# A fused attention and feed-forward layer: four engines' order inside one iteration laid out anew

## What is computed

```python
def layer(x):                      # heads: 16 of 32
    a = layernorm(x)
    Q, K, V = heads(a @ Wq.T + bq), heads(a @ Wk.T + bk), heads(a @ Wv.T + bv)
    scores = Q K^T / sqrt(32) - (i - j)      for j <= i, else -inf
    attn = softmax(scores) V @ Wo.T + bo
    x = x + layernorm(attn)
    xh = layernorm(x) @ hadamard(512)
    scale = clip(max|xh|, 1e-5) / 7          # per token
    xq = clip(round(xh / scale), -8, 7) * scale
    wq = ternary(weight) * mean|weight|      # per row
    return x + layernorm(xq @ wq.T)
```

## Time and profile before

| | |
|---|---|
| median of 3 runs | 1217.08 us (1214.96 to 1219.63) |
| profiled execution | 1213.31 us |
| its span | 1211.4 us |
| TensorE busy | 1100.2 us, 91% |
| VectorE busy | 1009.3 us, 83% |
| ScalarE busy | 702.7 us, 58% |
| GpSimd busy | 599.1 us, 49% |

### The profile page before, as it was taken

The page is one execution under the profiler, slowest core; times in us unless marked ns, Lnnn a source line. Parts: engine busy times, 40 slices in busy tenths (PEclk is TensorE's granted clock), DMA queues, the critical chain, the costliest instruction groups (busy, mean ns, idle before and its releaser), DMA issues.

```text
span 1211.4 us, 44874 instructions
## 1 busy us (share of the span) xinstructions
PE 1100.2 (91%) x18625; PEld 726.4 (60%) x18656; DVE 1009.3 (83%) x2558; ACT 702.7 (58%) x1494; POOL 599.1 (49%) x719
## 2 busy tenths in 40 slices
PE   5899999999999999999999999999999999999641
PEld 3566556666666666666566666666666666666320
DVE  5749998888988888899888888988888899887772
ACT  5454566666566566655666665566566655665431
POOL 2333545555454556555545555454556555445422
PEclk9999999999999999999999999999999999999875
DMA  9746665666666576566675656656575566654230
GB/s 271 165 110 138 124 130 136 159 138 136 134 125 137 142 146 153 125 136 138 122 145 137 159 134 137 136 125 132 142 149 145 131 137 138 124 129 102 72 70 36
DMA packets 204687, 161.81 MB, mean 134 GB/s; under 512 B 150432, under 2 KB 150688, under 8 KB 204384
## 3 DMA queue, kind: packets, MB, share of 16 engines
q1 hardware_dynamic: 199600, 141.34, 55.2%
q0 software_dynamic: 4880, 17.57, 4.1%
HBM read 40.87 MB, written 16.78 MB: 48 GB/s over the span
## 4 chain that ended last, share of the span: by engine, by line
PE 56%; DVE 32%; issue 7%; ACT 2%; SPq 1%; DMA 1%; POOL 1%; POOLq 0%; DVEq 0%; ACTq 0%
PE f_job L1281 42%; DVE f_bst L980 6%; PE f_st L1382 3%; DVE f_z L1058 3%; PE f_o L1399 2%; PE f_o L1404 2%; DVE f_o L970 2%; DVE f_inverse L972 2%; PE f_job L1426 2%; DVE f_rmax L948 2%; DVE f_x L1004 2%; DVE f_folded_x L1021 2%; DVE f_y L1012 2%; DVE f_y L1011 2%; DVE f_small L1006 1%
## 5 line engine op out<-in xcount | busy, mean ns | idle before, releaser
L469 POOL TENSOR_SCALAR_AFFINE_SELECT f_PT<-f_PT 64x512 f32<-64x512 f32 (+1 forms) x256 | 202.0, 810 | 68.6 <-ACT f_PT L635 42.8
L484 POOL TENSOR_TENSOR f_square<-f_stage 128x512 bf16<-128x512 f16 x128 | 130.8, 1044 | 130.7 <-ACT f_stage L613 117.5
L1281 PE MATMUL f_job<-f_xTh,f_wqh 128*128 128x256 f16 x512 | 140.8, 275 | 15.6 <-DVE f_wkl L809 14.4
L613 ACT ACTIVATE f_stage<-f_job,f_bias 128x256 f16<-128x256 f32 x256 | 106.0, 465 | 83.7 <-PE f_job L1281 76.9
L475 POOL TENSOR_TENSOR f_OTl<-f_o,f_OTh 128x256 f16<-128x256 f32 x128 | 86.3, 674 | 114.4 <-ACT f_OTh L653 113.6
L1281 PE MATMUL f_job<-f_xTl,f_wqh 128*128 128x256 f16 x512 | 140.2, 274 | 0.0
L1281 PE MATMUL f_job<-f_xTh,f_wql 128*128 128x256 f16 x512 | 140.2, 274 | 0.0
L1281 PE MATMUL f_job<-f_xTh,f_wkh 128*128 128x256 f16 x512 | 139.9, 273 | 0.0
L1281 PE MATMUL f_job<-f_xTh,f_wkl 128*128 128x256 f16 x512 | 139.8, 273 | 0.0
L1281 PE MATMUL f_job<-f_xTl,f_wkh 128*128 128x256 f16 x512 | 139.7, 273 | 0.0
L934 DVE SCALAR_TENSOR_TENSOR f_stage<-f_job,f_bias,f_stage 128x256 f16<-128x256 f32 x256 | 110.7, 474 | 29.5 <-ACT f_stage L613 27.5
(11 more groups left out here) (181 smaller groups left out, 3026.5 us busy)
## 6 DMA issues: line engine op xcount, KB each, us to landing
f_stacks<-f_stage SPq DMA_DIRECT2D x380, 128.0 KB
f_xin<-x SPq DMA_DIRECT2D x32, 512.0 KB, 4.6
f_x<-x SPq DMA_DIRECT2D x32, 512.0 KB, 4.0
out<-f_z POOLq DMA_DIRECT2D x32, 512.0 KB, 3.3
f_Vmix<-f_V SPq DMA_DIRECT2D x32, 256.0 KB, 3.2
f_Vmix<-f_V SPq DMA_DIRECT2D x64, 128.0 KB, 3.4
f_stacks<-rows_const SPq DMA_DIRECT2D x3, 512.0 KB, 7.8
f_stacks<-wqT SPq DMA_DIRECT2D x2, 512.0 KB, 6.0
```

Of the source, the lines that this page charges most:

```text
L469: nc.gpsimd.affine_select(out=d, in_=d, compare_op=ALU.is_ge, fill=0.0, base=odd * SUB, pattern=[[0, 4], [0, TP], [1, SUB]], channel_multi ...
L484: nc.gpsimd.tensor_tensor(square[:, 2 * m + pair, :], h, h, ALU.mult).then_inc(squared, 1)
L613: nc.scalar.activation(stage[:, 2 * m, g, :], bank("qk", g)[:, m * W2:(m + 1) * W2], ACT.Identity, bias=bias[:, m, g:g + 1]).then_inc(qk_h ...
L1281: mm = pe.matmul(dst, lhs[a](c), rhs[b](c), start=(n == 0), stop=(n == 3 * KC - 1))
```

## The change

It writes the loop bodies of SyncE, GpSimd, ScalarE and VectorE in another order. TensorE's list and all helpers stay as they are, so that every wait is the same and only its place in its engine's queue differs.

```diff
--- before.py
+++ after.py
@@ -411,23 +411,25 @@
             for s in range(STEPS - 1):
                 n, m, k = s + 1, s + 2, s - 1
                 max_rows(s)
+                if s < 2:
+                    load_rows(n)
                 if has(k):
                     load_res(k)
                 if has(m + 1):
                     load_front(m + 1)
-                if s < 2:
-                    load_rows(n)
+                if s:
+                    mix_values(s)
                 restack(n, 0)
                 restack(n, 1)
                 restack(n, 2)
                 if has(m):
                     turn_x(m)
-                mix_values(n)
                 if has(k):
                     turn_x2(k, 0)
                     turn_x2(k, 1)
 
             last = STEPS - 1
+            mix_values(last)
             max_rows(last)
             load_res(last - 1)
             turn_x2(last - 1, 0)
@@ -502,6 +504,8 @@
             for s in range(STEPS - 1):
                 n, m, k = s + 1, s + 2, s - 1
                 square_of(n, 0)
+                if s and has(k):
+                    heads_low(k, 2)
                 if has(k):
                     heads_low(k, 3)
                 if has(m):
@@ -518,15 +522,14 @@
                 if has(k - 1):
                     z_root(k - 1)
                 if has(s):
+                    heads_low(s, 0)
                     clear_future(s, 3)
-                    heads_low(s, 0)
                     heads_low(s, 1)
                 if has(k - 1):
                     finish_out(k - 1)
-                if has(s):
-                    heads_low(s, 2)
 
             last = STEPS - 1
+            heads_low(last - 1, 2)
             heads_low(last - 1, 3)
             clear_future(last, 0)
             clear_future(last, 1)
@@ -702,57 +705,60 @@
             keep_v(0, 1)
             for s in range(STEPS - 1):
                 n, m, k = s + 1, s + 2, s - 1
-                qk_high_part(n, 0)
                 if has(k):
                     invert(k, 3)
+                qk_high_part(n, 0)
+                if s:
+                    heads_high(k, 2)
                 qk_high_part(n, 1)
                 keep_max(s)
+                qk_high_part(n, 2)
                 if has(k):
                     heads_high(k, 3)
-                qk_high_part(n, 2)
+                if has(k - 1):
+                    round_levels(k - 1, 0)
+                qk_high_part(n, 3)
+                exps(s, 0, 0)
+                if has(k - 1):
+                    level(k - 1, 0)
+                exps(s, 0, 1)
                 if has(m):
                     front_norm(m, 0)
-                if has(k - 1):
-                    round_levels(k - 1, 0)
-                if has(m):
                     front_norm(m, 1)
-                qk_high_part(n, 3)
-                if has(k - 1):
-                    level(k - 1, 0)
-                exps(s, 0, 0)
-                exps(s, 0, 1)
+                    front_high(m)
                 if s == 0:
                     keep_ffscale()
-                    keep_tern()
-                if has(m):
-                    front_high(m)
                 exps(s, 1, 0)
                 exps(s, 1, 1)
                 if has(k - 1):
                     round_levels(k - 1, 1)
+                    keep_q(k - 1, 0)
+                if s == 0:
+                    keep_tern()
+                if has(k - 1):
                     level(k - 1, 1)
-                    keep_q(k - 1, 0)
                 invert(s, 0)
-                exps(s, 2, 0)
-                invert(s, 1)
                 if has(k - 1):
                     keep_q(k - 1, 1)
+                invert(s, 1)
+                exps(s, 2, 0)
+                heads_high(s, 0)
                 exps(s, 2, 1)
                 keep_v(n, 0)
-                if has(k):
-                    x2_high(k, 0)
-                    x2_high(k, 1)
-                heads_high(s, 0)
                 exps(s, 3, 0)
                 exps(s, 3, 1)
                 keep_v(n, 1)
+                if has(k):
+                    x2_high(k, 0)
+                invert(s, 2)
+                if has(k):
+                    x2_high(k, 1)
                 if has(k - 1):
                     norm_z(k - 1)
-                invert(s, 2)
                 heads_high(s, 1)
-                heads_high(s, 2)
 
             last = STEPS - 1
+            heads_high(last - 1, 2)
             keep_max(last)
             invert(last - 1, 3)
             heads_high(last - 1, 3)
@@ -1111,18 +1117,18 @@
                     front_stats(m)
                 if has(k - 1):
                     find_scale(k - 1, 0)
+                if s == 0:
+                    fold_bias()
+                qk_low_part(n, 2)
                 if has(m):
                     front_offset(m)
-                qk_low_part(n, 2)
+                if s < 4:
+                    weight_guard(s)
+                qk_low_part(n, 3)
                 if has(k - 1):
                     find_scale(k - 1, 1)
-                qk_low_part(n, 3)
-                if s == 0:
-                    fold_bias()
                 if has(k):
                     y_out(k, 0)
-                if s < 4:
-                    weight_guard(s)
                 if has(m):
                     front_low(m)
                 if has(k):
@@ -1131,32 +1137,31 @@
                 normalise(s, 0)
                 if has(k):
                     residual(k)
+                    fold(k, 0)
+                    fold(k, 1)
+                    fold_again(k, 0)
                 if has(k - 1):
                     scale_out(k - 1, 0)
-                if has(k):
-                    fold(k, 0)
-                    fold_again(k, 0)
-                    fold(k, 1)
-                    fold_again(k, 1)
-                if has(k - 1):
                     scale_out(k - 1, 1)
                     z_stats(k - 1)
                 if has(k):
+                    fold_again(k, 1)
+                maxima(n, 0)
+                keep_norms(n)
+                maxima(n, 1)
+                normalise(s, 1)
+                if has(k):
                     x2_low(k, 0)
-                normalise(s, 1)
-                maxima(n, 0)
-                maxima(n, 1)
-                keep_norms(n)
+                maxima(n, 2)
                 if has(k - 1):
                     z_columns(k - 1)
+                maxima(n, 3)
                 if has(k):
                     x2_low(k, 1)
-                maxima(n, 2)
-                maxima(n, 3)
                 split_max(n)
-                normalise(s, 2)
                 if has(k):
                     x_stats(k)
+                normalise(s, 2)
 
             last = STEPS - 1
             normalise(last - 1, 3)
```

## The result

| | before | after |
|---|---|---|
| median of the runs | 1216.7 us (4 runs beside the changed kernel) | 1178.1 us (1176.6 to 1181.4) |
| ratio, 95% interval | | 0.968 (0.965 to 0.971) |
| span of the profiled execution | 1211.4 us | 1177.6 us (its time 1179.3) |
| TensorE busy | | 1095.7 us, 93% |
| VectorE, ScalarE, GpSimd busy | | 84%, 60%, 50% |

What follows compares the result with a forecast made beforehand. TensorE was taken to wait for VectorE's unbroken queue, 1.74 us a step. Gains of 22.4 us (20 regular steps at 1.12), 4.4 (s = 2, 3) and 2.8 (boundary) make 29.6, from 1217.1 to 1187 us; range 1171 to 1208.

Steps and rivals of the forecast that it cites:

- The sign and the place: Faster, chance 0.80, by removing TensorE's wait at `values(n, 1)` for `scale_out` to empty its bank, 21.6 us in 29 waits.
- The folds and the start of the maxima: On VectorE, three folds take 2.04 us, the first `scale_out` starts at t0 + 7.58, `maxima(n, 0)` at t0 + 11.39.
- The present 0.46 stays in the sum: L1006 on VectorE still lasts 0.46 us over its best 0.148 us, as in its meeting with GpSimd's `clear_future(s, 2)`.
- the 0.23: Added to a regular step for GpSimd's clearings now falling on VectorE's folds: half of one clearing's 0.46 us.
- VectorE decides, by 0.13: At `out_product(k, 0)` VectorE is ready at 27.17 us, TensorE at 27.04, so VectorE sets the step at 33.48 us.
- rival A: TensorE alone decides the step, VectorE's queue is a little shorter and no meeting costs: 43.2 us gained, 1174 us, chance 0.12.
- The boundary steps: The 7 steps with softmax in more pieces gain 0.18 and 0.22 us each, 2.8 us together.
- s = 2 and s = 3: Two early steps also lose a longer wait for `scale_out`, since `weight_guard` moves: 2.15 + 2.2 = 4.4 us.
- Start and tail are unchanged: The first and last stretches of the kernel neither gain nor lose time.
- at nothing: SyncE's move of `mix_values` ahead of the next step's `restack` costs nothing, its reader coming only after t0.
- ScalarE, GpSimd: nothing: Moving the third head's parts, `x2_high` and `x2_low` later costs nothing, as long as ScalarE keeps its slack.
- Rivals B and C: VectorE pays for GpSimd meetings: B, two clearings, half given back, 1203 us, chance 0.20; C, four, slower, 1226 us, 0.11.

Runs made afterwards that it cites:

- run 3: The changed kernel with only both `scale_out` back at their old places among the folds: 1212.0 us, ratio 0.995.
- run 10: The changed kernel with both `scale_out` at their old places and GpSimd's clears of the third head cut from 64 to 4 columns of each block: 1188.9 us.
- run 4: The changed kernel with `normalise(s, 1)` ahead of both maxima again and `keep_norms` behind both: 1188.1 us, ratio 0.976.
- run 5: The changed kernel with SyncE's order of the kernel before, the rest as changed: 1173.4 us, ratio 0.965.
- run 6: The changed kernel with the last iteration's row of maxima issued ahead of the last `mix_values`, nothing else: 1175.0 us, ratio 0.966.
- run 8: The changed kernel with GpSimd's order of the kernel before, the rest as changed: 1179.4 us, ratio 0.970.
- run 1: The kernel before with the new order on VectorE alone: 1261.0 us, ratio 1.036.
- run 9: The kernel before with VectorE's new order and two of ScalarE's moves (both `front_norm`, both `x2_high`): 1214.5 us, ratio 0.997.
- run 2: The changed kernel with VectorE's order of before, the other three engines as changed: 1356.3 us, ratio 1.112.
- run 11: The changed kernel with one more `bn_stats` on VectorE in each iteration, ahead of the front's statistics: 1181.5 us, ratio 0.971.
- run 7: The changed kernel with the order of before in the first iterations alone, on VectorE, ScalarE and SyncE: 1181.6 us, ratio 0.970.

## Why the prediction was right, and where it was wrong

*The sign and the place*: right. The bank of `values(n, 1)` was the wait that fell, and runs 3 and 10 show that bringing the second `scale_out` forward is worth 0.5 us a step by its place alone, the maxima's order 0.47 (run 4).

*The folds and the start of the maxima*: the working of the three folds held (2.02 us against 2.04), and so did the distance from the first `scale_out` to `maxima(n, 0)`: 409.54 - 405.73 = 3.81 against 3.81.

*"The present 0.46 stays in the sum"* and the 0.23 added to it: this is the term that failed. `exps(s, 2, 1)` comes later, so the clearing no longer meets L1012 (0.15 instead of 0.61), and it starts behind a fold, so GpSimd pays. The prediction wrote that by the rule alone every clearing would stop a fold, and took half of one. But the rule of the Trainium skill that it names there (SBUF — State Buffer, section "SBUF: two separate sides") gives the ports to whichever starts first. Here the first fold was ahead by 0.54 us. The meeting that did become longer is another one, at the front's statistics: 0.82 where it was 0.51 before and the least of that line is 0.17. VectorE's way from one t0 (365.54) to the end of `qk_low_part(n, 2)` (392.27) is 26.73 us against a forecast of 27.12: 0.5 shorter up to the first maximum, 0.3 longer at the statistics; the other 0.2 I have not assigned.

*"VectorE decides, by 0.13"*: wrong, TensorE decides, though by no margin. Both arrive at `out_product(k, 0)` together, 26.79 us behind t0 (392.33 - 365.54), 0.06 us apart, and in all regular steps from s = 5 on but one (0.33) TensorE's idle time there is at most 0.14; forecast were 27.17 and 27.04. TensorE is 0.25 us earlier, mainly because the waits of 0.14 and 0.12 at `scores(n, 1)` and `scores(n, 3)` did not come. Where VectorE is 0.67 us earlier still, the step stays at 33.1 (run 5). The period forecast for a regular step was 33.48 before the 0.23; rival A said 33.09, and 33.02 to 33.11 came. Its sum of 43.2 us for the steady part stands against the measured 44.05. A margin of 0.13 us was smaller than what one meeting with GpSimd moves, and A deserved more than 0.12.

*The boundary steps* gained 0.55 each, not 0.40 (35.43 to 34.88); why 0.15 more is not shown. s = 2 and s = 3 together gained 6.0 us, not 4.4: they hold the regular gain twice, which was 1.12 in the sum and is 1.8, so this term fell short for the same reason.

*"Start and tail are unchanged"*: wrong, and this made the number look better than its terms. The steady part gained 44.05 us where the sum has 29.6, 14 us more, and the profiled execution lost 5.0 and 5.2 us at the ends; that the total came within 9 us of the forecast is two errors against each other, so in part luck. Run 6 shows the tail's: `mix_values(last)` was put ahead of the one transfer that TensorE waits for. Run 5 takes 2.2 us of that and about 1.9 us of the second step back; 1.5 us of the start's loss is the fall of the clock, which not every execution with this order shows. The prediction costed SyncE's move "at nothing" because it looked only at the regular step, where this is true.

*"ScalarE, GpSimd: nothing"*: GpSimd's move is worth nothing (run 8). ScalarE's earns nothing by itself either, but it is the condition of the gain. Runs 1 and 9 show VectorE's order without it at 1261 and 1214.5 us. What the prediction saw as one engine's change with company is one order on two engines; taking VectorE's half back costs 178 us (run 2).

*Rivals B and C*: the mechanism exists, at the size given (0.95 for a pair of clearings, run 3), but it struck no fold here. Without the order of the folds ahead of `scale_out` it would have.

**The better version.** Runs 5 and 6 have medians 4.7 and 3.1 us under the changed kernel's. The intervals of the ratios overlap with its own (0.963 to 0.967 and 0.964 to 0.968, against 0.965 to 0.971), so the times alone do not prove it for run 6; all five times of run 5 (1171.2 to 1175.2) lie below all four of the changed kernel (1176.6 to 1181.4). The traces say where the difference comes from. The spans, 1171.4 and 1171.3 against 1177.6, overstate it, in part by the clock at the start of the latter. SyncE's order of before with the other three engines' new one is the version to keep: 1173.4 us.

## What to carry to other kernels

Where engines hand work round in a circle, an order belongs to all of them: judge a move by where its readers on the other queues ask for it. Here half of the change was worse than none (runs 1 and 2) or no better (run 9). Where two instructions of VectorE and GpSimd may meet, write down which starts first, to a tenth of a microsecond; in these traces that decided who paid. Before a span is set against another, compare the granted clock stretch by stretch: two executions of the same first steps differed by 3.4 us. A queue laid out for the regular step has to be read once more for the first iterations and the last, where the transfer that stands first is the one that somebody waits for.

## What the runs showed of the hardware that I had not expected

- One meeting of VectorE and GpSimd costs either side, by 0.5 us in who starts first: the same folds and the same pair of clearings took 0.42 each and 2.71 in the changed kernel, 0.92, 0.87 and 1.50 in run 3.
- An instruction of 0.6 us more on VectorE can cost nothing because it moves the next one out of a meeting of 0.59 us (run 11).
- A GpSimd instruction that came second waited for a whole row of VectorE instructions: the first clearing of the changed kernel's pair took 2.08 us, until all six fold instructions were through.
- With waits of TensorE of about 3 us in each step its granted clock fell to half for 3.4 or 6.8 us, 28 times in run 2, with 51 us more of busy time for the same instructions. One fall of 3.4 us in the second step cost 1.5 us.
- The load of the constants' rows took 10.5 us to land when issued behind seven other DMAs and right before the twelve of `restack` (run 7), and 4.9 when only the two of the row of maxima stood ahead.
